# Token choice of a state-space and attention block: scores spread by a repeated column, ranks added in one operation, one-hot rows in one comparison

## The chip, the cores and the metric

The kernel runs on one core of a Trainium2 chip (trn2). A core has a matrix engine (PE, with its weight loads listed apart as PEld), VectorE (DVE), ScalarE (ACT), GpSimd (POOL) and SyncE (SP, which here only issues transfers), an on-chip memory SBUF of 128 partitions, and the accumulators PSUM in 8 banks. The engines run their own instruction streams in program order and wait for each other on semaphores. The metric is the device time of one execution in microseconds (us); lower is better.

## What is computed

The input has 4 batches of 512 tokens with 256 features. The first half is a selective state-space layer with 16 states per channel, followed by a layer norm; the second half picks 64 of the 512 tokens of each batch by a router score, runs attention and an MLP over the 256 picked tokens, puts them back, and ends with another layer norm. Cut to what matters for the change:

```
x = layernorm(x + ssm(x))                       # the scan: h = dA * h + dBu, 16 states
scores = einsum('btd,d->bt', x, w_router)       # [4, 512]
_, idx = top_k(scores, 64); idx = sort(idx)     # 64 tokens of each batch, in token order
sel = x[b, idx]                                 # [256, 256], then attention and MLP on it
output = x.at[b, idx].set(gated)
x = layernorm(x + output)
```

The kernel has no sort. A token is picked when fewer than 64 tokens of its batch rank ahead of it; its place among the picked ones is the count of picked tokens in front of it; a 0/1 matrix (the one-hot rows, token by place) then gathers rows by a matmul.

## The kernel before

A batch has 4 chunks (C = 4) of 128 tokens, one token per partition. The scan runs as a loop of 64 steps t, 16 for each of the 4 batches, one state per step. In a step PE turns two blocks of the scan's input into PSUM (`turn_bu`, line 538) and sums weighed states (`add_states`, line 675); ACT makes the decays (line 1037) and most of the scan's input (line 1027); DVE runs two scans of 512 tokens (line 1186); POOL weighs the states (`weigh`, line 1565, 128x1024) and in every second step makes a part of the scan's input (`make_z`, line 1578).

Between these, hand-written tables put the pieces of other work. `FRONT_AT` puts the preparation of the next batch (convolution, projections) into the steps of the current one, and `TAIL_AT` puts the tail of the batch before: its output projection (o0, o1), layer norm (ls, lp, la), router scores (lx), the spreading of scores (ld, sb), ranks (k0 to k3), places (pf), and the gather (ga, and for every second batch the position tables, cs). So the tails of batches 0, 1 and 2 run inside the scan of batches 1, 2 and 3, and the tail of batch 3 (`LAST_TAIL`) runs after the loop, mixed with the first query and key projections (q0 to q11: PE line 699, DVE lines 1329 and 1334, POOL line 1594) and value projections (v0, v1: PE line 709). Each engine takes the pieces in the same order, each piece at its place in that engine's stream.

The pieces that the change touches, in the order in which a tail runs them:

- lx0, lx1 (DVE, line 1250): four sums of products with the router's weights, one for each chunk. They write the scores into column 256 of the chunk's rows in `x1`, and raise `x1_ready` after two chunks and after four.
- ld0, ld1 (POOL, line 1625): four 128x128 diagonal matrices, the identity times a chunk's score column, into `score_diag`; each raises `diag_ready`.
- sb (PE, line 628): two matmuls of all ones with two diagonals each (128x256). Their result in a PSUM bank has on every partition all 512 scores of the batch.
- k0 to k3 (DVE, lines 1263 to 1267): for each chunk up to three comparisons of the 512 scores with the chunk's own, summed into `ranks`, which has three rows of four numbers per partition. Chunk 0 has no number in the first row, so that one is kept at zero.
- The end of k3 (DVE, lines 1274 to 1280): two additions give the rank, `chosen` is 1 where it is below 64 (this releases pf on PE), `offset` is 0 or 1000, and a memset puts the zero back.
- pf (PE, lines 632 and 635, DVE, lines 1284 and 1288): eight records of small matmuls on `chosen` count the picked tokens in front, DVE adds `offset` to make `place`, and four comparisons of `slot_no` (0 to 63) with a chunk's `place` make the one-hot rows, 128x64 each.
- ga, cs (PE, lines 641 and 647): the gather, and the cosines and sines of the picked positions.

Between k3 and pf DVE has the two scans of the next step. PE's queue is in program order too: what stands behind a waiting piece waits with it.

Of the kernel before, what the change touches and what calls it, by code (L numbers as in the profile page):

```python
# [51 lines left out]
FIRST_BU = ("cv0c", "cv0d")  # L52
TAIL_AT = {
    2: ("y0", "y1", "g0", "g1"), 4: ("o0",), 5: ("o1",), 6: ("ls0", "ls1"), 7: ("lp0", "lp1"),
    8: ("la0", "la1"), 9: ("lx0", "lx1", "ld0", "ld1"), 10: ("sb",), 11: ("k0",), 12: ("k1",), 13: ("k2", "k3"),
    14: ("pf",), 15: ("ga", "cs"),
}

# [2 lines left out]
NORM_AT = {5: "hs", 6: "hp", 7: "hr", 8: "ht"}  # L61
LAST_TAIL = (
    "y0", "y1", "g0", "g1", "q0", "q1", "o0", "q2", "ls0", "q3", "lp0", "ls1", "q4", "o1", "lp1", "q5", "q6",
    "la0", "la1", "lx0", "lx1", "ld0", "ld1", "q7", "q8", "sb", "k0", "k1", "k2", "k3", "v0", "q9", "q10", "pf",
    "q11", "ga", "v1", "cs",
)
NO_FILL = (
    "su", "s1", "s2", "s3", "s4", "s5", "s6", "rs", "y0", "y1", "g0", "g1", "ls0", "ls1",
    "la0", "la1", "lp0", "lp1", "lx0", "lx1", "ld0", "ld1", "k0", "k1", "k2", "k3",
)  # L70


# [19 lines left out]
def block_kernel(nc, x, W_in, conv_w, conv_b, W_x, W_dt, b_dt, A_log, D, W_out, w_router, wq, bq, wk, bk, wv, bv,  # L92
# [115 lines left out]
    with ExitStack() as ctx:  # L208
        def sb(name, shape, dt=F32):
            return ctx.enter_context(nc.sbuf_tensor(name, shape, dt))  # L210
# [112 lines left out]
        x1 = sb("x1", [P, B * C, NCOL])  # L323
        junk = sb("junk", [P, 2, L], BF16)
        h_buf = sb("h", [P, ST * DM + KD * S])
        score_diag = sb("score_diag", [P, C, P])
        ranks = sb("ranks", [P, 3, C])
        offset = sb("offset", [P, C])
        chosen = sb("chosen", [P, C])
        place = sb("place", [P, C])  # L330
# [31 lines left out]
        total = loop_buf[:, FC * S:FC * S + B * C * DM].rearrange("p (b c d) -> p b c d", b=B, c=C)  # L362
        out_rows = total
        selT = gT_buf[:].rearrange("p (t l) -> p t l", t=ST)
        change = score_diag[:].rearrange("p a b -> p (a b)").rearrange("p (t d) -> p t d", t=ST)
        h_rows = h_buf[:, 0:ST * DM].rearrange("p (t d) -> p t d", t=ST)
        hT = h_buf[:, ST * DM:].rearrange("p (k s) -> p k s", k=KD)

# [35 lines left out]
        rstd_ready = sem("rstd_ready")  # L404
        rows_ready = sem("rows_ready")
        x1_ready = sem("x1_ready")
        diag_ready = sem("diag_ready")
        chosen_ready = sem("chosen_ready")
        onehot_ready = sem("onehot_ready")
        sel_stat = sem("sel_stat")  # L410
# [125 lines left out]
        def _(pe):  # L536
# [68 lines left out]
            def tail(b, piece):  # L605
                o = int(piece[-1]) if piece[-1].isdigit() else 0
                name = (piece, b)
                if piece in NO_FILL or (piece == "cs" and b % 2 == 0):
                    return
                wait_free(pe, name)  # L610
                t = at(name)
                if piece in ("o0", "o1"):
                    pe.wait_ge(in_w["w_out"], 16)
                    pe.wait_ge(g_ready, 2 * b + o + 1)
                    pe.wait_ge(res_ready, b + 1)
                    for i in range(2):
                        cols = slice((2 * o + i) * P, (2 * o + i + 1) * P)
                        for k in range(KD):
                            mm = pe.matmul(t[:, i * DM:(i + 1) * DM], gT[:, k, cols], w_out_s[:, k, :],  # L619
                                           start=(k == 0), stop=(k == KD - 1))  # L620
                        for k in range(KD):
                            a = i * DM + k * P
                            mm = pe.matmul(t[:, a:a + P], resT[b % 2][:, k, cols], ident[:], start=False,
                                           stop=True, skip_group_check=True)
                elif piece == "sb":
                    for i in range(2):
                        pe.wait_ge(diag_ready, C * b + 2 * (i + 1))
                        mm = pe.matmul(t[:, 2 * P * i:2 * P * (i + 1)], ones[:],
                                       score_diag[:, 2 * i:2 * i + 2, :].rearrange("p c j -> p (c j)"), start=True, stop=True)
                elif piece == "pf":  # L630
                    pe.wait_ge(chosen_ready, b + 1)
                    mm = pe.matmul(t[:, 0:C], before[:], chosen[:], start=True, stop=True)
                    for w in range(1, C):

                        mm = pe.matmul(t[:, w:C], ones[:], chosen[:, 0:C - w], start=False, stop=True,
                                       skip_group_check=True)
                elif piece == "ga":
                    pe.wait_ge(onehot_ready, C * (b + 1))
                    r = K * (b % 2)
                    for c in range(C):  # L640
                        mm = pe.matmul(t[r:r + K, 0:NCOL], onehot[:, b // 2, c, r:r + K], x1[:, C * b + c, :],  # L641
                                       start=(c == 0), stop=(c == C - 1))
                elif piece == "cs":
                    pe.wait_ge(tables, 4)
                    for i, tab in enumerate((cos_tab, sin_tab)):
                        for c in range(C):
                            mm = pe.matmul(t[:, i * P:(i + 1) * P], tab[:, c, :], onehot[:, b // 2, c, :],
                                           start=(c == 0), stop=(c == C - 1))
                fill_done(name, mm)
# [520 lines left out]
        def _(dve):  # L1170
# [60 lines left out]
            def tail(b, piece):  # L1231
# [21 lines left out]
                elif piece in ("k0", "k1", "k2", "k3"):  # L1253
# [17 lines left out]
                        return  # L1271
                    drain_done(name, ins)
                    wait_drained(dve, name)
                    link(dve.tensor_tensor(ranks[:, 0, :], ranks[:, 0, :], ranks[:, 1, :], ALU.add))
                    link(dve.tensor_tensor(ranks[:, 2, :], ranks[:, 0, :], ranks[:, 2, :], ALU.add))
                    dve.tensor_scalar(chosen[:], ranks[:, 2, :], float(K), None, ALU.is_lt).then_inc(chosen_ready, 1)

                    dve.wait_ge(chosen_ready, b + 1)
                    link(dve.tensor_scalar(offset[:], chosen[:], -1000.0, 1000.0, ALU.mult, ALU.add))
                    link(dve.memset(ranks[:, 0, 0:1], 0.0))  # L1280
                elif piece == "pf":

                    wait_filled(dve, name)
                    drain_done(name, dve.tensor_tensor(place[:], at(name)[:, 0:C], offset[:], ALU.add))
                    wait_drained(dve, name)
                    r = K * (b % 2)
                    for c in range(C):
                        dve.tensor_scalar(onehot[:, b // 2, c, r:r + K], slot_no[:], place[:, c:c + 1], None,
                                          ALU.is_equal).then_inc(onehot_ready, 1)

            def layer_norm_stats(rows, first, signal, slot=0):

# [210 lines left out]
        def _(pool):  # L1503
# [93 lines left out]
            def tail(b, piece):  # L1597
# [9 lines left out]
                elif piece in ("lp0", "lp1"):  # L1607
# [3 lines left out]
                    if b >= 1:  # L1611
# [3 lines left out]
                    link(inv_sqrt(rstd[:, 0, chunks], var, LN_EPS))  # L1615
                    pool.tensor_tensor(shift[:, 0, chunks], shift[:, 0, chunks], rstd[:, 0, chunks], ALU.mult)\
                        .then_inc(rstd_ready, 1)
                elif piece in ("ld0", "ld1"):
                    o = int(piece[-1])

                    pool.wait_ge(x1_ready, 2 * b + o + 1)
                    if b >= 1:
                        wait_filled(pool, ("sb", b - 1))
                    for c in range(2 * o, 2 * o + 2):
                        pool.tensor_scalar(score_diag[:, c, :], ident[:], x1[:, C * b + c, DM:DM + 1], 1.0,
                                           ALU.mult, ALU.mult).then_inc(diag_ready, 1)

            for piece in FIRST_FRONT:
                front(0, piece)
# [63 lines left out]
```

## Time and profile before

| | us |
|---|---|
| three timed runs | 489.69, 491.65, 491.72 (median 491.65) |
| the profiled execution | 488.78 |
| its span, first to last instruction | 487.0 |
| PE busy | 413.7 (85%) |
| DVE busy | 313.9 (64%) |
| ACT busy | 294.4 (60%) |
| POOL busy | 284.9 (59%) |

The profile is of one execution. A row of the timeline gives a start, a length, the engine, the line, what is written and read with its shape and count, and in brackets how long the engine had been idle before and what released it. Neighbouring rows of one kind are merged, and a row's end can overlap the next one's start a little, since an operation's last results are still under way. An operation that is held by the hardware after its start shows the wait in its length, not in the brackets. Busy shares are means over stages with different limits, so the reading goes by stage: scan loop to about 345 us, last tail to 384, projections to 399, attention to 447, then MLP and output.

### The profile page before, as it was taken

What the parts mean: (1) busy time and instruction counts of PE and PEld (TensorE: products, weight loads), DVE (VectorE), ACT (ScalarE), POOL (GpSimd) and SP (SyncE); (2) the same over time, 40 slices, a digit from 0 to 9 for tenths busy, and PEclk for the clock granted to TensorE, in tenths of its full rate; (3) what the DMA queues carried; (4) which work ended last, traced back from release to release, by engine and by line L of the source; (5) the groups of instructions that cost most, each with busy time, mean ns of one, the idle gap of its engine ahead of it and who ended that gap; (6) DMA issues with size and microseconds to landing.
All of it is one profiled execution on the core that took longest, in us unless ns stands there. A gap on an engine that the chain in (4) does not pass through costs nothing.

```text
span 487.0 us, 6491 instructions
## 1 busy us (share of the span) xinstructions
PE 413.7 (85%) x2021; PEld 249.4 (51%) x2021; DVE 313.9 (64%) x624; ACT 294.4 (60%) x628; POOL 284.9 (59%) x261
## 2 busy tenths in 40 slices
PE   5989898899999799899875789866968998999991
PEld 3433353444445344446333346342755777888881
DVE  0302664588665579973689967999489396544355
ACT  4255588994786993676795376971252465553152
POOL 2010086678987889777889769996562253331012
PEclk9999999999999979999989699977997899999996
DMA  7102501106101004111002204870400000000013
GB/s 235 44 0 72 148 23 31 34 2 160 59 24 42 23 0 93 64 43 42 7 18 67 89 25 157 250 282 0 174 0 1 2 0 1 3 0 1 1 44 129
DMA packets 18709, 29.10 MB, mean 60 GB/s; under 512 B 2698, under 2 KB 10676, under 8 KB 18420
## 3 DMA queue, kind: packets, MB, share of 16 engines
q1 hardware_dynamic: 18676, 28.70, 19.1%
q8 instruction: 16, 0.26, 0.2%
q14 instruction: 17, 0.14, 0.1%
HBM read 22.27 MB, written 2.23 MB: 50 GB/s over the span
## 4 chain that ended last, share of the span: by engine, by line
PE 45%; ACT 15%; DVE 12%; POOL 8%; issue 8%; POOLq 0%; DVEq 0%; ACTq 0%
PE bank L538 8%; PE bank L554 7%; ACT loop_buf L1027 6%; ACT front_a L1037 5%; PE bank L675 4%; POOL state L1565 3%; PE bank L851 3%; PE bank L827 3%; PE bank L619 2%; PE bank L641 2%; DVE state L1186 2%; PE bank L859 1%; PE bank L576 1%; PE bank L798 1%; PE bank L818 1%
## 5 line engine op out<-in xcount | busy, mean ns | idle before, releaser
L1186 DVE TENSOR_TENSOR_SCAN state<-front_a,bank 128x512 f32<-128x512 f32 x88 | 102.6, 1204 | 42.9 <-PE bank L538 21.3
L538 PEld LDWEIGHTS bank<-ident,loop_buf 128*128 128x128 f32 x512 | 60.4, 146 | 83.5 <-issue 40.1
L538 PE MATMUL bank<-ident,loop_buf 128*128 128x128 f32 x512 | 84.8, 290 | 17.2 <-ACT loop_buf L1027 15.4
L1037 ACT ACTIVATE front_a<-loop_buf,a_neg 128x512 f32<-128x512 f32 x128 | 84.4, 713 | 7.9 <-DVE copy L1186 4.8
L1027 ACT ACTIVATE loop_buf<-copy,b_rows 128x256 f32<-128x256 f32 x190 | 78.9, 496 | 0.1
L554 PE MATMUL bank<-front_c,conv_raw 128*128 128x512 f32 x128 | 60.7, 607 | 2.5 <-ACT front_c L902 0.9
L1186 DVE TENSOR_TENSOR_SCAN copy<-front_a,bank 128x512 f32<-128x512 f32 x40 | 47.1, 1207 | 23.8 <-PE bank L538 8.4
L1565 POOL TENSOR_TENSOR state<-state,front_a 128x1024 f32<-128x1024 f32 x22 | 52.2, 2375 | 9.0 <-DVE state L1186 9.0
L1565 POOL TENSOR_TENSOR state<-state,c_own 128x1024 f32<-128x1024 f32 x22 | 51.9, 2361 | 9.2 <-DVE state L1186 9.0
L675 PE MATMUL bank<-state,fold 128*64 128x512 f32 x176 | 50.7, 656 | 1.5 <-POOL state L1565 1.5
L1578 POOL TENSOR_TENSOR loop_buf<-copy,b_rows 128x512 f32<-128x512 f32 x31 | 33.4, 1079 | 24.4 <-ACT copy L902 21.9
L554 PEld LDWEIGHTS bank<-front_c,conv_raw 128*128 128x128 f32 x128 | 23.0, 195 | 22.9 <-issue 20.8
L1594 POOL TENSOR_TENSOR loop_buf<-state 128x256 f32<-128x256 f32 x24 | 17.5, 732 | 28.0 <-DVE state L1334 28.0
L1538 POOL TENSOR_TENSOR copy<-front_c,front_b 128x1024 f32<-128x1024 f32 x4 | 8.0, 1996 | 35.5 <-ACT front_b L902 30.6
L902 ACT ACTIVATE front_b<-bank,vec 128x512 f32<-128x512 f32 x16 | 10.9, 682 | 29.4 <-PE bank L554 26.3
L902 ACT ACTIVATE copy<-bank 128x512 f32<-128x512 f32 x20 | 11.6, 594 | 27.5 <-PE bank L538 15.3
L1565 POOL TENSOR_TENSOR copy<-copy,c_own 128x1024 f32<-128x1024 f32 x10 | 23.9, 2387 | 5.6 <-DVE copy L1186 5.2
L699 PE MATMUL bank<-h,copy 128*128 128x128 f32 x192 | 23.9, 279 | 1.4 <-ACT h L1044 0.9
L699 PEld LDWEIGHTS bank<-h,copy 128*128 128x128 f32 x192 | 22.5, 193 | 4.3 <-issue 3.0
L1565 POOL TENSOR_TENSOR copy<-copy,front_a 128x1024 f32<-128x1024 f32 x10 | 24.6, 2462 | 0.0
L675 PE MATMUL bank<-copy,fold 128*64 128x512 f32 x80 | 22.5, 641 | 0.4 <-POOL copy L1565 0.4
L1329 DVE SCALAR_TENSOR_TENSOR state<-bank,vec,cosT 128x128 f32<-128x128 f32 x48 | 14.3, 339 | 8.6 <-ACT state L1060 8.5
(205 smaller groups left out, 745.9 us busy)
## 6 DMA issues: line engine op xcount, KB each, us to landing
front_a<-c_stage SPq DMA_DIRECT2D x32, 128.0 KB, 2.9
c_own<-c_stage SPq DMA_DIRECT2D x32, 128.0 KB, 2.8
loop_buf<-front_b SPq DMA_DIRECT2D x32, 128.0 KB, 2.3
copy<-in_L_attn_x SPq DMA_DIRECT2D x4, 512.0 KB, 3.8
front_b<-in_L_ffn_wo SPq DMA_DIRECT2D x1, 2048.0 KB, 10.0
copy<-in_L_ffn_wq SPq DMA_DIRECT2D x1, 2048.0 KB, 8.3
out<-loop_buf SPq DMA_DIRECT2D x3, 512.0 KB, 3.0
conv_raw<-in_L_attn_conv_w SPq DMA_DIRECT2D x2, 512.0 KB, 3.8
```

Of the source, the lines that this page charges most:

```text
L538: return pe.transpose(dst, src, ident[:])
L554: mm = pe.matmul(at(name)[:], conv_x[:, k, i, o * P:(o + 1) * P], xT[:, i, k:k + L], start=(j == 0), stop=(j == TAPS * KD - 1))
L675: mm = pe.matmul(bank[Y_BANK[h]][j * P // 2:(j + 1) * P // 2, :], fold[:], state[t % NH][:, j, :], start=(m == 0), stop=(m == NPAIR - 1))
L699: mm = pe.matmul(at(name)[:, i * P:(i + 1) * P], w_qk[:, k, head * P:(head + 1) * P], hT[:, k, p * P:(p + 1) * P], start=(k == 0), stop=(k ...
L827: mm = pe.matmul(at(("wo", p))[:, 0:DM], oT[:, h, p * P:(p + 1) * P], w_o[:, h, :], start=(h == 0), stop=(h == N_HEADS - 1))
L902: drain_done(name, act.activation(dst, at(name)[:] if src is None else src, func, **kw))
L1027: act.activation(zed[:, g % NZ, c, :, i, :], du_rows[b % 2][:, c, :].rearrange("p (k d) -> p k d", k=2 * KD), ACT.Copy, scale=b_rows[:, b ...
L1037: act.activation(decay[:, u % NDA, :], delta_wide[:, b % 2, k, :], ACT.Exp, scale=a_neg[:, k, m:m + 1]).then_inc(decay_made, 1)
L1186: dve.tensor_tensor_scan(state[t % NH][:, j, :], decay[:, u % NDA, :], bank[BU_BANK[u % NBU]][:], 0.0, ALU.mult, ALU.add).then_inc(scanned, 1)
L1565: pool.tensor_tensor(state[t % NH], state[t % NH], c_wide[g % NCW].unsqueeze(1).to_broadcast([P, 2, L]), ALU.mult).then_inc(weighed, 1)
L1578: pool.tensor_tensor(zed[:, g % NZ, c], rows, cols, ALU.mult).then_inc(z_pool, 1)
L1594: pool.tensor_tensor(qkT[:, 2 * j:2 * j + 2, p * P:(p + 1) * P], qk_raw[:, i0 % NQK], qk_swap[:, i0 % NQK], ALU.add).then_inc(roped, 1)
```

## The change

- The four diagonal matrices of a tail and their pieces ld0 and ld1 go, on POOL. PE makes the spread scores itself: in place of two matmuls of ones with diagonals (128x256) there are four with the score column, read 128 times over with a step of zero, as the stationary operand and the identity as the moving one (128x128 each). PE now waits for `x1_ready`, the scores themselves.
- The two additions of the ranks become one reduction over the three rows of `ranks`, into a tile of its own (`rank_sum`). The zero is then never overwritten, and the memset that restored it goes.
- The four comparisons that make one-hot rows become one, over 128 x 4 x 64, with both operands repeated by steps of zero; it raises `onehot_ready` once.
- `change`, which shared the diagonals' memory, gets a tile of its own. Nothing else reads that memory.

```diff
-    8: ("la0", "la1"), 9: ("lx0", "lx1", "ld0", "ld1"), 10: ("sb",), ...
+    8: ("la0", "la1"), 9: ("lx0", "lx1"), 10: ("sb",), ...
...
                 elif piece == "sb":
-                    for i in range(2):
-                        pe.wait_ge(diag_ready, C * b + 2 * (i + 1))
-                        mm = pe.matmul(t[:, 2 * P * i:2 * P * (i + 1)], ones[:],
-                                       score_diag[:, 2 * i:2 * i + 2, :].rearrange("p c j -> p (c j)"), start=True, stop=True)
+                    for c in range(C):
+                        pe.wait_ge(x1_ready, 2 * b + c // 2 + 1)
+                        mm = pe.matmul(t[:, c * P:(c + 1) * P], x1[:, C * b + c, DM:DM + 1].to_broadcast([P, P]), ident[:],
+                                       start=True, stop=True)
...
                 elif piece == "ga":
-                    pe.wait_ge(onehot_ready, C * (b + 1))
+                    pe.wait_ge(onehot_ready, b + 1)
...
-                    link(dve.tensor_tensor(ranks[:, 0, :], ranks[:, 0, :], ranks[:, 1, :], ALU.add))
-                    link(dve.tensor_tensor(ranks[:, 2, :], ranks[:, 0, :], ranks[:, 2, :], ALU.add))
-                    dve.tensor_scalar(chosen[:], ranks[:, 2, :], float(K), None, ALU.is_lt).then_inc(chosen_ready, 1)
+                    link(dve.tensor_reduce(rank_sum[:], ranks[:].rearrange("p a c -> p c a"), AX.X, ALU.add))
+                    dve.tensor_scalar(chosen[:], rank_sum[:], float(K), None, ALU.is_lt).then_inc(chosen_ready, 1)
...
-                    link(dve.memset(ranks[:, 0, 0:1], 0.0))
...
-                    for c in range(C):
-                        dve.tensor_scalar(onehot[:, b // 2, c, r:r + K], slot_no[:], place[:, c:c + 1], None,
-                                          ALU.is_equal).then_inc(onehot_ready, 1)
+                    shape = [P, C, K]
+                    dve.tensor_tensor(onehot[:, b // 2, :, r:r + K], slot_no[:].unsqueeze(1).to_broadcast(shape),
+                                      place[:].unsqueeze(2).to_broadcast(shape), ALU.is_equal).then_inc(onehot_ready, 1)
...
-                elif piece in ("ld0", "ld1"):
-                    o = int(piece[-1])
-
-                    pool.wait_ge(x1_ready, 2 * b + o + 1)
-                    if b >= 1:
-                        wait_filled(pool, ("sb", b - 1))
-                    for c in range(2 * o, 2 * o + 2):
-                        pool.tensor_scalar(score_diag[:, c, :], ident[:], x1[:, C * b + c, DM:DM + 1], 1.0,
-                                           ALU.mult, ALU.mult).then_inc(diag_ready, 1)
```

DVE at the end of the ranks in batch 1's tail, between the scans of batch 2 (line 1186), before and then after:

```order
L1267 SCALAR_TENSOR_TENSOR junk,ranks<-bank,x,earlier 128x128
L1274 TENSOR_TENSOR ranks<-ranks 128x4
L1275 TENSOR_TENSOR ranks<-ranks 128x4
L1276 TENSOR_SCALAR chosen<-ranks 128x4
L1279 TENSOR_SCALAR offset<-chosen 128x4
L1280 MEMSET ranks 128x1
L1186 SCALAR_TENSOR_TENSOR copy<-front_a,bank 128x512 x2
L1284 TENSOR_TENSOR place<-bank,offset 128x4
L1288 TENSOR_SCALAR onehot<-slot_no,place 128x64 x4
```

```order
L1267 SCALAR_TENSOR_TENSOR junk,ranks<-bank,x,earlier 128x128
L1274 TENSOR_REDUCE rank_sum<-ranks 128x4
L1275 TENSOR_SCALAR chosen<-rank_sum 128x4
L1278 TENSOR_SCALAR offset<-chosen 128x4
L1186 SCALAR_TENSOR_TENSOR copy<-front_a,bank 128x512 x2
L1282 TENSOR_TENSOR place<-bank,offset 128x4
L1286 TENSOR_TENSOR onehot<-slot_no,place 128x4x64
```

The scans stand where they stood; five instructions ahead of them are three, and the four behind `place` are one.

POOL in batch 2's tail, in the scan of batch 3, before and then after (line numbers are two lower after):

```order
L1565 TENSOR_TENSOR state<-state,front_a 128x1024
L1578 TENSOR_TENSOR loop_buf<-copy,b_rows 128x512
L1625 TENSOR_SCALAR score_diag<-ident,x 128x128 x4
L1565 TENSOR_TENSOR state<-state,front_a 128x1024
L1565 TENSOR_TENSOR copy<-copy,front_a 128x1024
```

```order
L1563 TENSOR_TENSOR state<-state,front_a 128x1024
L1576 TENSOR_TENSOR loop_buf<-copy,b_rows 128x512
L1563 TENSOR_TENSOR state<-state,front_a 128x1024
L1563 TENSOR_TENSOR copy<-copy,front_a 128x1024
```

The weighing of the next step follows directly on the make_z, with no wait for the scores between.

## Rows read from the trace of the kernel before

**Rows 1.** Page, part 4: the chain that ended last, by engine.
```profile
PE 45%; ACT 15%; DVE 12%; POOL 8%; issue 8%; POOLq 0%; DVEq 0%; ACTq 0%
```
**Rows 2.** Table by stretch: length; busy PE, PEld, DVE, ACT, POOL; clock; DMA; GB/s.
```profile
272.00:280.00 8.00, 5.77 (x15) 2.45 (x15) 7.96 (x10) 1.45 (x2) 5.07 (x4) 0.50 0.22 78
```
**Rows 3.** Timeline of DVE, batch 0's tail: start, length, line, operation, idle before.
```profile
196.27 4.79 DVE L1288 TENSOR_SCALAR onehot<-slot_no,place 128x64 f32<-128x64 f32 x4
```
**Rows 4.** Timeline of POOL, batch 0's tail.
```profile
174.12 1.04 POOL L1547 TENSOR_SCALAR front_c<-front_c 128x1024 f32<-128x1024 f32 x1 [1.52 <-ACT front_b L981]
...
195.17 2.36 POOL L1565 TENSOR_TENSOR copy<-copy,c_own 128x1024 f32<-128x1024 f32 x1
```
**Rows 5.** Timeline of PE, batch 0's tail.
```profile
177.14 1.13 PE L628 MATMUL bank<-score_diag,ones 128*128 128x256 f32 x4
...
201.21 1.92 PE L641 MATMUL bank<-x,onehot 128*64 128x257 f32 x8 [1.65 <-DVE onehot L1288]
```
**Rows 6.** Timeline of DVE, batch 1's tail.
```profile
263.91 1.46 DVE L1274 TENSOR_TENSOR ranks<-ranks 128x4 f32<-128x4 f32 x1
265.40 2.29 DVE L1275 TENSOR_TENSOR ranks<-ranks 128x4 f32<-128x4 f32 x1
...
270.05 0.96 DVE L1279 TENSOR_SCALAR offset<-chosen 128x4 f32<-128x4 f32 x1
...
271.22 2.33 DVE L1186 TENSOR_TENSOR_SCAN copy<-front_a,bank 128x512 f32<-128x512 f32 x2
...
273.64 3.67 DVE L1288 TENSOR_SCALAR onehot<-slot_no,place 128x64 f32<-128x64 f32 x4
```
**Rows 7.** Timeline of POOL, batch 1's tail.
```profile
262.99 2.35 POOL L1557 TENSOR_TENSOR copy<-front_b,copy 128x1024 f32<-128x1024 f32 x1
...
273.70 2.40 POOL L1565 TENSOR_TENSOR copy<-copy,c_own 128x1024 f32<-128x1024 f32 x1 [0.40 <-PE bank L538]
...
279.63 2.34 POOL L1565 TENSOR_TENSOR copy<-copy,c_own 128x1024 f32<-128x1024 f32 x1 [2.53 <-DVE copy L1186]
285.01 2.37 POOL L1565 TENSOR_TENSOR state<-state,front_a 128x1024 f32<-128x1024 f32 x1 [3.04 <-DVE state L1186]
```
**Rows 8.** Timeline of PE, batch 1's tail.
```profile
277.46 3.66 PE L641 MATMUL bank<-x,onehot 128*64 128x257 f32 x8 [1.94 <-DVE onehot L1288]
...
282.11 1.06 PE L647 MATMUL bank<-onehot,sin_tab 128*128 128x128 f32 x8
```
**Rows 9.** Timeline of DVE, batch 2's tail.
```profile
315.77 2.57 DVE L1250 CUSTOM_DVE_ANT_0 junk<-x,router 128x256 bf16<-128x256 f32 x1
...
319.45 0.42 DVE L1250 CUSTOM_DVE_ANT_0 junk<-x,router 128x256 bf16<-128x256 f32 x1
...
336.92 2.83 DVE L1288 TENSOR_SCALAR onehot<-slot_no,place 128x64 f32<-128x64 f32 x4
```
**Rows 10.** Timeline of POOL, batch 2's tail.
```profile
319.22 1.84 POOL L1625 TENSOR_SCALAR score_diag<-ident,x 128x128 f32<-128x128 f32 x4
```
**Rows 11.** Timeline of PE, batch 2's tail.
```profile
339.90 3.06 PE L641 MATMUL bank<-x,onehot 128*64 128x257 f32 x7 [2.35 <-DVE onehot L1288]
```
**Rows 12.** Timeline of DVE, last tail.
```profile
366.75 0.75 DVE L1265 TENSOR_SCALAR_CACHE_REDUCE z<-bank,x 128x512 bf16<-128x512 f32 x1 [0.30 <-PE bank L628]
...
371.06 0.16 DVE L1274 TENSOR_TENSOR ranks<-ranks 128x4 f32<-128x4 f32 x1
...
372.04 0.61 DVE L1329 SCALAR_TENSOR_TENSOR state<-bank,vec,cosT 128x128 f32<-128x128 f32 x2
...
374.55 1.30 DVE L1288 TENSOR_SCALAR onehot<-slot_no,place 128x64 f32<-128x64 f32 x4
```
**Rows 13.** Timeline of PE, last tail.
```profile
376.00 2.89 PE L641 MATMUL bank<-x,onehot 128*64 128x257 f32 x8 [2.21 <-DVE onehot L1288]
```
**Rows 14.** DVE groups by form: count, busy us, mean ns, idle before.
```profile
L1295 DVE BATCH_NORM_STATS2 stats<-z 128x6 f32<-128x256 f32 x16 | 5.8, 406 | 1.2 <-ACT z L902 1.2
...
L1421 DVE TENSOR_TENSOR state<-state,sel 128x256 f32<-128x256 f32 x2 | 0.8, 424 | 0.0
```

More of the change, by code:

```diff
@@ L54 @@
     2: ("y0", "y1", "g0", "g1"), 4: ("o0",), 5: ("o1",), 6: ("ls0", "ls1"), 7: ("lp0", "lp1"),
-    8: ("la0", "la1"), 9: ("lx0", "lx1", "ld0", "ld1"), 10: ("sb",), 11: ("k0",), 12: ("k1",), 13: ("k2", "k3"),
+    8: ("la0", "la1"), 9: ("lx0", "lx1"), 10: ("sb",), 11: ("k0",), 12: ("k1",), 13: ("k2", "k3"),
     14: ("pf",), 15: ("ga", "cs"),
@@ L63 @@
     "y0", "y1", "g0", "g1", "q0", "q1", "o0", "q2", "ls0", "q3", "lp0", "ls1", "q4", "o1", "lp1", "q5", "q6",
-    "la0", "la1", "lx0", "lx1", "ld0", "ld1", "q7", "q8", "sb", "k0", "k1", "k2", "k3", "v0", "q9", "q10", "pf",
+    "la0", "la1", "lx0", "lx1", "q7", "q8", "sb", "k0", "k1", "k2", "k3", "v0", "q9", "q10", "pf",
     "q11", "ga", "v1", "cs",
@@ L68 @@
     "su", "s1", "s2", "s3", "s4", "s5", "s6", "rs", "y0", "y1", "g0", "g1", "ls0", "ls1",
-    "la0", "la1", "lp0", "lp1", "lx0", "lx1", "ld0", "ld1", "k0", "k1", "k2", "k3",
+    "la0", "la1", "lp0", "lp1", "lx0", "lx1", "k0", "k1", "k2", "k3",
 )
@@ L325, in block_kernel @@
         h_buf = sb("h", [P, ST * DM + KD * S])
-        score_diag = sb("score_diag", [P, C, P])
+        change_buf = sb("change", [P, ST * DM])
         ranks = sb("ranks", [P, 3, C])
+        rank_sum = sb("rank_sum", [P, C])
         offset = sb("offset", [P, C])
@@ L364, in block_kernel @@
         selT = gT_buf[:].rearrange("p (t l) -> p t l", t=ST)
-        change = score_diag[:].rearrange("p a b -> p (a b)").rearrange("p (t d) -> p t d", t=ST)
+        change = change_buf[:].rearrange("p (t d) -> p t d", t=ST)
         h_rows = h_buf[:, 0:ST * DM].rearrange("p (t d) -> p t d", t=ST)
@@ L406, in block_kernel @@
         x1_ready = sem("x1_ready")
-        diag_ready = sem("diag_ready")
         chosen_ready = sem("chosen_ready")
```

## Prediction

> **What bounds the kernel now.** I read the page's chain first: no engine holds it; PE has 45%, the others take turns [rows 1]. So the question is, for each of the four tails, who waits for the pieces that change. For that I read the timelines of DVE, POOL and PE side by side around each tail, looking at idle times in brackets and at operations far longer than their work.
>
> Two things stand out. First, in all four tails PE stands idle in front of the gather, released by DVE's one-hot rows: 1.65, 1.94, 2.35 and 2.21 us [rows 5, 8, 11, 13]. Second, small DVE operations take the time of a POOL operation. A 128x4 addition took 0.16 us in the last tail [rows 12] and 2.29 us in batch 1's, where POOL was working without a pause; the first addition there ends, at 265.4, when POOL's operation from 262.99 does (265.34) [rows 6, 7]. The four comparisons should take well under 1 us; they took 4.79, 3.67, 2.83 and 1.30 [rows 3, 6, 9, 12]. Each such operation seems to wait until the POOL operation then running ends, and POOL's next one goes ahead of DVE's next: one POOL operation (about 2.35 us for a weighing) for each DVE operation. Not every DVE operation is held: the bn_stats of the same loop, one SBUF input of 256, mean 406 ns over 16 of them, which leaves no room for a hold [rows 14]. So the count of held DVE operations is the price, and the change lowers it.
>
> In batch 1's tail this is the bound: DVE is 7.96 of 8 us busy from 272 to 280 while PE, ACT and POOL wait [rows 2], and POOL, which paces the loop after it, is idle 0.40, 2.53 and 3.04 us, each time released by DVE or PE [rows 7].
>
> **Batch 0's tail.** Removed: four comparisons. Added: one, 128x256 with two SBUF inputs. Its nearest row is a 128x256 tensor_tensor, 0.42 us [rows 14]. It may be held once: the POOL operation running when the comparisons began at 196.27 ends at 195.17 + 2.36 = 197.53 [rows 3, 4], so it is done by 197.95 where the fourth was done at 201.06. PE was free at 201.21 - 1.65 = 199.56 [rows 5], so the gather starts then: **1.65 us**, all of PE's wait and no more. PE holds the chain behind it, so I let this carry through. The diagonals were free here: POOL had another 1.52 us to wait for ACT after them [rows 4]. The two saved additions are worth little here, since DVE had slack until the gather.
>
> **PE's new matmuls.** Four 128x256 records took 1.13 us at full clock [rows 5]; the new piece has eight of 128x128, and eight such took 1.06 [rows 8]. I cost it at nothing. The column read with a step of zero as a weight load has no row; above, I bound it by twice the nearest streaming time (1 us more for a tail, of which only batch 0's and the last would be on the path), below by nothing.
>
> **Batch 1's tail.** From 263.91 to 271.22 DVE spends 7.3 us on five tiny operations, four of them held [rows 6]. After, the reduction takes some 0.2 us if it isn't held, and two held ones are left: `chosen` is done when the first addition was (265.4) and `offset` when the second was (267.7). DVE goes on at 267.8, 3.4 earlier. The two scans (2.25) bring it to 270.1, and the single comparison, held for at most 2.40 [rows 7], ends between 270.6 and 273.0 where the fourth ended at 277.3. PE's gather, which began at 277.46, can begin at 273.1 at the latest: 4.4 earlier. If the shorter gap keeps PE's clock up, the gather itself falls from 3.66, at a granted clock of 0.50 (1.2 GHz), to 1.92 [rows 2, 5, 8], 1.7 more. Behind it POOL becomes late: it has only 0.40 + 2.53 + 3.04 = 5.97 us of idle time to give back [rows 7]. So 4.4 to 6.0. Should the reduction be held as the addition was, everything up to the one-hot is one operation (2.3) later: 4.4 - 2.3 = 2.1. Ends 2.1 and 6.0; I take **5.3**, since bn_stats, the nearest row for a reduction along the free axis, is not held.
>
> The Trainium skill ("SBUF — State Buffer", Who interferes with whom) says that on trn2 tensor_reduce never contends with GpSimd, while tensor_scalar and a tensor_tensor with two SBUF inputs do. The held rows here agree; no run shows a reduction from SBUF yet. By that rule the lower end is 4.4, not 2.1.
>
> **Batch 2's tail.** Here POOL's diagonals stood on the chain: 1.84 us [rows 10]. But DVE's four router sums overlap them, and they are held too: 2.57 against 0.42 us for the fourth, which ran at 319.45 beside the diagonals [rows 9]. Without these, POOL starts the next weighing at 319.2, and by the alternation the fourth sum waits for it: 2.35 us later, and DVE with three scans behind it is the later engine from there. So the removal is not a gain but a loss: **-2.35** if held (nearest: the second sum), 0 if it slips in. Then the rank part, unheld: two operations fewer, 0.4 us (five take 0.98 in the last tail [rows 12]). Then the comparison: POOL is idle there, waiting for the scan; the first of four ran at once and the rest waited for the weighing it let start. A single one goes at once: 2.83 - 0.42 = 2.4, and PE's wait was 2.35 [rows 9, 11]. Sum -2.35 + 0.4 + 2.4 = **0.45**; ends 2.8 (sum not held) and -1.95 (the comparison held as well).
>
> **Last tail.** PE's spread no longer waits for POOL, but DVE, busy with query projections until then, had waited just 0.30 us [rows 12]; that is all that can be gained there. The rank part saves 0.4. The comparisons: 1.30 becomes 0.42, or some 1.0 if held by the short POOL addition that held the first: 0.3 to 0.9. Sum 1.0 to 1.6; I take **1.2**. PE's wait of 2.21 covers it [rows 13], and the stage behind starts from PE, so it carries to the end.
>
> Against the merging speaks the Trainium skill ("VectorE: DVE Perf Modes", The perf-mode tier table): fp32 tensor_scalar streams two elements a cycle, tensor_tensor one. By its 0.96 GHz that is, as an estimate, 0.13 us more streaming for 256 elements. The rows decide otherwise: the operations cost mostly what is fixed and what holds them, not the streaming.
>
> **The sum.** 1.65 + 5.3 + 0.45 + 1.2 = 8.6 us. Against the profiled execution (488.78, span 487.0 and 1.8 around it) that is 480.2; that execution lay 2.9 below the median of the timed runs. From the median, 491.65 - 8.6 = 483.0, which I forecast.
>
> **Rivals.**
> - *Slower: the sums collide everywhere.* In batches 0 and 1 too POOL could run on into its next work once the diagonals are gone, and DVE's four router sums would be held as in batch 2: some 2 us each, 8 a tail, 16 for two tails. It decides at line 1547, which follows the diagonals: for it POOL must be free of its wait for ACT, which lasted 1.52 us past the diagonals in batch 0 [rows 4]. Against: that wait is ACT's, and the change does nothing for ACT. Time: 491.65 - 8.6 + 16 = 499.
> - *Given back in the loop.* ACT or PE turns out to pace the scan, so that what tails 0 and 1 free is waited for elsewhere; 0.45 + 1.2 remain: 490.0. Against: POOL's idle times name DVE and PE as releasers. For: ACT and PE hold much of the chain between the tails.
> - *The low ends.* The reduction is held (2.1), the sum and the comparison in batch 2 are both held (-1.95), and the last gives 1.0: 1.65 + 2.1 - 1.95 + 1.0 = 2.8, so 488.9. The part of the change that adds ranks then does little of what it should.
> - *The high ends.* 1.65 + 6.0 + 2.8 + 1.6 = 12.05: 479.6.
>
> **How the numbers follow.** Forecast 0.53 (481 to 486), high ends 0.18, low ends 0.14, given back 0.11, collision 0.04. A measurement tells about 0.5%, 2.5 us, from no change; the forecast, the high ends and most of the low ones lie beyond. Faster 0.81, same 0.15, slower 0.04. The range of 8 in 10 leaves out the collision and what is given back, and takes in most of the low ends and, for the 2.9 between profile and median, a little beyond the high ones: 478.5 to 488.5.
>
> **What would show it.** Per tail in the profile after: no wait of PE in front of batch 0's gather; in batch 1 a reduction of 0.2 us and two held operations behind it, POOL's idle sum of 6 us nearly gone; in batch 2 a fourth router sum over 2 us long, and the comparison at its bare 0.4; in the last tail a gather some 1.2 us nearer to the end of the scan. Wrong it would be if the reduction takes 2 us beside POOL, if the column's weight loads take much over 0.25 us, or if POOL's idle times reappear further on.

## The result, and the profile after

The changed kernel takes 476.25 us (median of 6 runs, 473.71 to 479.89) where the kernel before, on the same chip, has 490.85. The ratio is 0.9706, 95% interval 0.9648 to 0.9765: 14.6 us less. In a second comparison it was 0.9718 (0.9686 to 0.9751), 13.7 us. Medians here and below are of all executions; ratios and their intervals are of those within 1.5% of the fastest execution of the same kernel. The forecast was 8.6 us less, and its range ended at 478.5: the direction is right, the size too small. The profiled execution took 478.12 (span 476.4, mean clock 0.952) beside 488.78 (487.0, 0.943).

DVE of the changed kernel in the four tails, answering [rows 3, 6, 9, 12] (start, length, line, operation, idle before):

```profile
198.64 1.70 DVE L1286 TENSOR_TENSOR onehot<-slot_no,place 128x256 f32<-128x256 f32 x1
...
264.87 0.17 DVE L1274 TENSOR_REDUCE rank_sum<-ranks 128x4 f32<-128x12 f32 x1
265.07 0.99 DVE L1275 TENSOR_SCALAR chosen<-rank_sum 128x4 f32<-128x4 f32 x1
266.10 2.29 DVE L1278 TENSOR_SCALAR offset<-chosen 128x4 f32<-128x4 f32 x1
...
271.54 0.42 DVE L1286 TENSOR_TENSOR onehot<-slot_no,place 128x256 f32<-128x256 f32 x1
...
313.47 2.55 DVE L1250 CUSTOM_DVE_ANT_0 junk<-x,router 128x256 bf16<-128x256 f32 x1
...
332.17 0.43 DVE L1286 TENSOR_TENSOR onehot<-slot_no,place 128x256 f32<-128x256 f32 x1
...
366.35 0.42 DVE L1286 TENSOR_TENSOR onehot<-slot_no,place 128x256 f32<-128x256 f32 x1
```

In batch 1 the reduction is not held, and the two small operations behind it are. The single comparison is held once, in batch 0, and takes its bare 0.42 us, as [rows 14] had it, in the other three. The fourth router sum of batch 2 is long, where it took 0.42 before.

POOL of the changed kernel, answering [rows 7], with the DVE scans that wait for PE behind batch 1's gather:

```profile
263.67 2.36 POOL L1555 TENSOR_TENSOR copy<-front_b,copy 128x1024 f32<-128x1024 f32 x1
...
271.60 2.59 POOL L1563 TENSOR_TENSOR state<-state,c_own 128x1024 f32<-128x1024 f32 x1
274.14 2.35 POOL L1563 TENSOR_TENSOR copy<-copy,c_own 128x1024 f32<-128x1024 f32 x1
...
277.63 3.44 DVE L1186 TENSOR_TENSOR_SCAN state<-front_a,bank 128x512 f32<-128x512 f32 x3 [2.31 <-PE bank L538]
...
285.97 2.51 POOL L1604 TENSOR_TENSOR gT<-gT,copy 128x512 f32<-128x512 f32 x2 [0.49 <-DVE gT L1239]
...
366.39 0.97 POOL L1592 TENSOR_TENSOR loop_buf<-state 128x256 f32<-128x256 f32 x1 [0.55 <-DVE state L1332]
```

From 263.67 to 285.5 POOL has no idle time left. PE has none from 266.18 to 279.6 either, and DVE's scans wait 2.31 us for it: both engines are full in this stretch now.

PE's four gathers and the projection behind the last, answering [rows 5, 8, 11, 13]:

```profile
201.90 1.90 PE L641 MATMUL bank<-x,onehot 128*64 128x257 f32 x8
...
273.27 1.90 PE L641 MATMUL bank<-x,onehot 128*64 128x257 f32 x8
...
332.74 2.78 PE L641 MATMUL bank<-x,onehot 128*64 128x257 f32 x7
...
366.92 1.92 PE L641 MATMUL bank<-x,onehot 128*64 128x257 f32 x8 [1.16 <-DVE onehot L1286]
368.78 1.98 PE L709 MATMUL bank<-front_c,h 128*128 128x512 f32 x4
```

Three of the four waits for DVE's one-hot rows are gone. And the gathers are shorter themselves: 1.90 for 3.66 in batch 1, 1.92 for 2.89 in the last tail, where the projection took 2.66 before. That is PE's clock: the granted clock over the gather was 0.50 in batch 1 and 0.64 in the last tail (0.74 over the projection), and it is 1.00 over all three now. Batch 2's gather is still at 0.64. PE's 32 weight loads from the repeated column took 185 to 338 ns (median 191) where the 16 from `ones` took 186 to 337 (median 238): no price.

Where the time went, tail by tail, from the starts of the same scan operation (line 1186) in both traces, and from the end:

| stretch | forecast | changed, profiled |
|---|---|---|
| to the first scan (58.51 before, 61.07 after) | 0 | -2.6 |
| batch 0's tail | 1.65 | 1.84 |
| batch 1's tail | 5.3 | 6.68 |
| batch 2's tail | 0.45 | 1.35 |
| last tail | 1.2 | 3.3 |
| the tails together | 8.6 | 13.2 |

The first row isn't the change. It comes and goes between executions: the rank part alone, which touches nothing there, started its first scan at 61.09, and one of the kernels below that holds the whole change, at 58.73. A second profiled execution of the changed kernel (475.64 us) gave 3.4, 7.1, 1.4 and 3.3 us in the four tails, so a tail can differ by 1.6 between executions. The question is why the tails gave 13.2 and not 8.6.

The chain of the page names less than half of the span now, so its shares can't be set beside [rows 1] one by one; PE still holds the most of it:

```profile
PE 23%; DVE 10%; ACT 5%; POOL 3%; issue 3%; POOLq 0%; DVEq 0%; ACTq 0%
```

### The profile page after: what moved, and what is told of

The parts are those of the page before. It is cut to its first block and busy times, and to the rows that moved or that the text cites. A ratio compares the mean times of both kernels' runs of the same rounds, so it can differ in the third digit from the quotient of the medians.

```text
span 476.4 us, 6481 instructions
## 1 busy us (share of the span) xinstructions
PE 413.1 (87%) x2037; PEld 250.5 (53%) x2037; DVE 302.2 (63%) x604; ACT 294.5 (62%) x628; POOL 278.7 (59%) x245
## 5 line engine op out<-in xcount | busy, mean ns | idle before, releaser
L538 PE MATMUL bank<-ident,loop_buf 128*128 128x128 f32 x512 | 85.0, 291 | 16.2 <-ACT loop_buf L1027 14.6
```

What stands on the lines that cost most here:

```text
L538: return pe.transpose(dst, src, ident[:])
```

## The experiments

### Each part alone, and each part undone

The diff has three parts that can be applied one by one: the rank addition (lines 1274 to 1280), the single comparison (line 1288), the spread scores without diagonals (lines 628 and 1625).

Rank part alone:

```
-  ranks0 += ranks1; ranks2 += ranks0; chosen = ranks2 < K; ...; memset
+  rank_sum = tensor_reduce(ranks); chosen = rank_sum < K; ...
```

> The kernel before with the rank part alone: one reduction for two additions, no memset. Theory (a DVE operation on two SBUF inputs, or a comparison of SBUF data, is held until POOL's running operation ends; a reduction is not): in batch 1's tail chosen and offset stay held, the scan behind them starts 3.4 us earlier, the four comparisons are still held; batch 2 and the last tail gain 0.4 each. 3 to 5 us faster than before. Rival (the reduction is held like the addition): its row in batch 1's tail is over 1 us long and the gain is 1 to 2 us.

Measured: 490.95, ratio 0.9992 (0.9963 to 1.0022). A miss: nothing is gained that can be measured. Its trace, batch 1's tail, DVE, then POOL and PE:

```profile
265.55 0.17 DVE L1275 TENSOR_REDUCE rank_sum<-ranks 128x4 f32<-128x12 f32 x1
265.75 1.17 DVE L1276 TENSOR_SCALAR chosen<-rank_sum 128x4 f32<-128x4 f32 x1
266.95 2.28 DVE L1279 TENSOR_SCALAR offset<-chosen 128x4 f32<-128x4 f32 x1
269.27 2.33 DVE L1187 TENSOR_TENSOR_SCAN copy<-front_a,bank 128x512 f32<-128x512 f32 x2
...
272.39 5.97 DVE L1287 TENSOR_SCALAR onehot<-slot_no,place 128x64 f32<-128x64 f32 x4
```

```profile
271.49 1.03 POOL L1577 TENSOR_TENSOR loop_buf<-copy,b_rows 128x512 f32<-128x512 f32 x1
272.49 2.35 POOL L1564 TENSOR_TENSOR state<-state,c_own 128x1024 f32<-128x1024 f32 x1
274.81 2.33 POOL L1564 TENSOR_TENSOR copy<-copy,c_own 128x1024 f32<-128x1024 f32 x1
277.11 1.03 POOL L1577 TENSOR_TENSOR loop_buf<-copy,b_rows 128x512 f32<-128x512 f32 x1
...
278.50 3.66 PE L642 MATMUL bank<-x,onehot 128*64 128x257 f32 x8 [3.93 <-DVE onehot L1287]
```

Up to the scan it went as forecast, 3.5 us sooner. But DVE now comes to the four comparisons when POOL has four operations in a row: the comparisons took 5.97 us, 2.3 more than before [rows 6], and end at 278.36, where POOL's fourth ends at 278.14. PE waits 3.93 us for them. What was saved on held additions was spent on held comparisons.

Single comparison alone:

```
-  for c in range(C): tensor_scalar(onehot[:, c], slot_no, place[:, c], is_equal)
+  tensor_tensor(onehot, slot_no repeated, place repeated, is_equal)
```

> The kernel before with the single comparison alone. Theory: batch 0's gather loses its wait of 1.65 us; batch 1's rank part stays as long as before (7.3 us) and the one-hot rows come 3.3 us earlier; batch 2 gains 2.4, with the diagonals still there and so no held fourth router sum; the last tail gains 0.9, and up to 1.5 more if PE's clock stays up for the gather. 7 to 10 us faster. Rival (the parts are worth something only together, since POOL or ACT paces batch 1): under 5 us.

Measured: 479.49, ratio 0.9763 (0.973 to 0.9796), 11.3 us; more than expected, and what the excess is was not followed up.

Spread scores alone:

```
-  ld0, ld1: POOL score_diag = ident * score; PE sb: ones x score_diag, 128x256 x4
+  PE sb: (score column repeated) x ident, 128x128 x8
```

> The kernel before with the spreading of scores alone (no diagonals, the column as stationary operand). Theory: nothing in batches 0 and 1; in batch 2 the fourth router sum is held by a weighing (2.5 us long instead of 0.42), which costs 2.1 us; the last tail gains 0.45. So 1 to 2.5 us slower than before. Rival (the diagonals stood on the chain, 1.84 us in batch 2, and PE's wait of 4.78 us in the last tail was theirs): 2 to 5 us faster.

Measured: 492.49, ratio 1.0037 (1.0004 to 1.0071): a loss of about 1.7, as expected.

The whole change once more, in the same comparison:

> The whole change, beside its parts on the same chip. By the theory the parts add up nearly: 3 to 5, 7 to 10 and -1 to -2.5, so 10 to 13 us faster than before; the first measurement had 14.6. Rival (the parts need each other): the whole is over 3 us more than the sum of the parts measured beside it.

Measured: 477.05, ratio 0.9718 (0.9686 to 0.9751), as expected, 13.7 us. The parts alone sum to 9.4: some 4 us belong to no part alone. So each was undone from the changed kernel. Four comparisons back:

> The changed kernel with the four comparisons back (ranks by one operation and spread scores stay). Theory (whatever time DVE saves ahead of them, the four comparisons lose again, since each waits for one of POOL's operations): nothing is left of the change, 490 to 493, with a one-hot of 5 to 6 us in batch 1's tail where the changed kernel has 0.42. Rival (the parts simply add): the single comparison's 11.3 go and the rest stays, 488 or a little less.

Measured: 492.08, ratio 1.0001 (0.9972 to 1.0029). As the theory has it: without the single comparison nothing is left. (Its profiled execution was the shortest of its 12; the one-hot of batch 1 took 4.58 us there, under the expected 5 to 6.) The old rank additions back:

> The changed kernel with the rank additions back (single comparison and spread scores stay). Theory (with the single comparison the two held additions are a loss of their own): batch 1's scan resumes some 3.4 us later than in the changed kernel, of which POOL's idle time behind covers a part; 479.5 to 481, about 2.5 to 4 over the changed kernel. Rival (rank part worth nothing as it is alone): 476.5 to 477.5.

Measured: 479.67, ratio 0.9756 (0.9724 to 0.9788): by the medians 2.6 to 3.4 us over the changed kernel, as the theory has it. DVE in its batch 1:

```profile
262.36 1.18 DVE L1274 TENSOR_TENSOR ranks<-ranks 128x4 f32<-128x4 f32 x1
263.57 2.28 DVE L1275 TENSOR_TENSOR ranks<-ranks 128x4 f32<-128x4 f32 x1
265.89 2.29 DVE L1276 TENSOR_SCALAR chosen<-ranks 128x4 f32<-128x4 f32 x1
268.21 0.96 DVE L1279 TENSOR_SCALAR offset<-chosen 128x4 f32<-128x4 f32 x1
...
271.80 0.42 DVE L1288 TENSOR_TENSOR onehot<-slot_no,place 128x256 f32<-128x256 f32 x1
```

Four held operations ahead of the scan, one free comparison behind it. The diagonals back (rank part and single comparison together):

> The rank part and the single comparison together, the scores spread by POOL's diagonals as before. Alone they were worth -0.2 and 11.3 us. Theory (the rank part's gain needs the single comparison: with four, the time saved on held additions is lost again on comparisons held by POOL's work, 5.97 us against 3.67): together they give 11.3 and some 2.5 to 3 for batch 1's tail, and the spreading is a loss also here (2.15 in batch 2, less 0.3 and 0.4): 475 to 476, a little under the whole change. Rival (the rank part gives nothing, and the whole change's extra over the sum of its parts came with the spreading): 479 to 480.

Measured: 477.41, ratio 0.9704 (0.9646 to 0.9762): 1.4 to 2.4 more than expected, and the same as the whole change. Beside the other two, the spreading is worth nothing that can be measured. So the rank part is worth 0 alone and 2 to 3 us with the single comparison. By the ratios it is 0.9756 beside 0.9706 and 0.9718 (1.9 to 2.5 us), and 0.9763 beside 0.9704 (2.9 us). The intervals of each pair overlap, but all 12 executions with the single comparison alone or with the spread scores have a mean of 479.7, and the 16 that have the rank part too 476.9. In the traces, batch 1's tail gives 3.7 us with the old additions and 6.7 without.

### The router sums of batch 2

The prediction put 2.35 us of loss on the fourth router sum, held by the weighing that the missing diagonals let start sooner. Two kernels make POOL wait for the sums, with one line in its tail, the first ahead of the weighing after the make_z, the second two operations earlier:

```
+  if b == 2: pool.wait_ge(x1_ready, 2 * (b + 1))
```

> The changed kernel with one wait more: in batch 2's tail POOL starts the weighing that follows the make_z only when all four router sums are there. Theory (the fourth sum is held by that weighing, a loss of 2.15 us in the changed kernel): the sum takes 0.4 us instead of 2.55, the scan behind it comes some 2.1 us sooner, and POOL, which stands idle 2.68 us two operations later, loses nothing: about 474.5 where the changed kernel has 476 to 477. Rival (the sum is long because of PE's new reads of the same score columns, not because of POOL): it stays at 2.5 us and the time at 476 to 477.

> The changed kernel with the same wait put two POOL operations earlier, so that in batch 2's tail the third and fourth sums and mostly the second too run with POOL idle. Theory: each of them then takes 0.4 instead of 2.57, 1.25 and 2.55 us, DVE is through the four some 5 us sooner, and the scan behind them with it; POOL starts two operations up to 1.5 us later, for which its idle 2.68 and 0.60 us pay. 471.5 to 473. Rival (POOL, held back by the wait, becomes what the scan waits for): no more than one hold is won, 474 to 475.5.

DVE and POOL with the first wait, then DVE, POOL and PE with the second:

```profile
313.33 0.41 DVE L1250 CUSTOM_DVE_ANT_0 junk<-x,router 128x256 bf16<-128x256 f32 x1
...
313.83 2.36 POOL L1563 TENSOR_TENSOR state<-state,front_a 128x1024 f32<-128x1024 f32 x1 [0.71 <-DVE x L1250]
```

```profile
305.51 0.41 DVE L1250 CUSTOM_DVE_ANT_0 junk<-x,router 128x256 bf16<-128x256 f32 x1
...
305.86 0.41 DVE L1250 CUSTOM_DVE_ANT_0 junk<-x,router 128x256 bf16<-128x256 f32 x1
...
306.20 0.41 DVE L1250 CUSTOM_DVE_ANT_0 junk<-x,router 128x256 bf16<-128x256 f32 x1
...
306.70 2.37 POOL L1563 TENSOR_TENSOR state<-state,front_a 128x1024 f32<-128x1024 f32 x1 [1.40 <-DVE x L1250]
...
320.41 2.28 DVE L1278 TENSOR_SCALAR offset<-chosen 128x4 f32<-128x4 f32 x1
...
325.71 3.23 PE L641 MATMUL bank<-x,onehot 128*64 128x257 f32 x7 [2.31 <-DVE onehot L1286]
...
360.51 3.40 PE L641 MATMUL bank<-x,onehot 128*64 128x257 f32 x8 [1.16 <-DVE onehot L1286]
```

The sums are as the theory has them: 0.41 instead of 2.55, and in the second kernel three times 0.41. The scan behind them starts 2.1 and 5.1 us sooner than in the changed kernel, counted from the last scan ahead of them. The times don't show it: 477.88 (0.969, 0.961 to 0.9771) and 477.3 (0.9718, 0.9652 to 0.9783), the same as the changed kernel. In the second kernel's trace 2.4 of the 5.1 go in the ranks, above all because `offset` is held again, 2.28 us, where POOL had been idle in the changed kernel. Another 0.7 goes at batch 2's gather, 3.23 us for seven matmuls, which at the 0.24 of each of batch 0's eight [rows 5] would be 1.7, and 1.5 at the last tail's, 3.40 where the changed kernel has 1.92. At the end 0.7 is left. In the first kernel's trace 1.3 of the 2.1 go around batch 2's gather, and 0.8 is left at the end. The granted clock over the second kernel's two gathers was 0.50 and 0.56: that pointed to the clock.

### PE's clock

The records give each execution's mean clock. From 36 runs of the kernel before it was 0.945, that is (1 - 0.945) x 2 x 491 = 54 us at the lower of the two levels (1.2 GHz); 12 of the changed kernel had 0.957, 41.5 us. To see what that is worth, PE was kept busy: matmuls of the identity with itself, put in front of PE's waits into a bank that is overwritten next.

```
+  for i in range(n): pe.matmul(bank, ident, ident)   # ahead of the wait
```

First in the kernel before, last tail alone:

> The kernel before with more work for PE and nothing else: in the last tail 18 matmuls of 128x128 ahead of the spread scores and 8 ahead of the gather, in PE's idle times of 4.78 and 2.21 us; their results are overwritten. Theory (of the 3.3 us that the last tail gave, 1.5 are PE's clock: gather 2.89 and the projection behind it 2.66 us where full clock takes 1.92 and 1.98): with PE kept busy both fall to the lower figures and the time by about 1.5 us, 489 beside 490.75. Rival (the clock follows something else): both stay long, 490.75 or a little above.

Measured: 491.0, ratio 0.9992 (0.9956 to 1.0029). A miss in time. In the profiled execution gather and projection did fall, to 2.17 and 1.98 us, but the eight in front of the gather took 3.33 us, the low stretch fell on them (granted clock 0.55), and they ended 1.0 us after the one-hot rows were there. Then in all tails, in both kernels:

> The kernel before with more work for PE and nothing else: 128x128 matmuls (3 to 16 at a place, of about 0.23 us) that fill PE's waits of 1.4 to 4.8 us in front of the spread, the ranks and the gather of all batches and in front of batch 2's du; results are overwritten. The clock in the records says that 36 executions of the kernel before had a mean clock of 0.945, 54 us at the low level, and 12 of the changed kernel 0.957, 41.5 us; within one kernel's executions 1 us less of it goes with 0.15 to 0.45 us less time. Theory (the share of the gain that the sum of operations lacks is PE's clock, kept up by the shorter waits): low time falls by 15 to 25 us and the time by 3 to 6: 485 to 488 beside 491. Rival (the low clock lies beside other work that sets the end): 490 to 492.

> The changed kernel with its own remaining waits of PE filled in the same way (batch 2's du, and spread, ranks and gather of the tails of batches 2 and 3; 3 to 9 matmuls at a place). Theory: low time falls from some 41 to about 25 us and the time by 2 to 4: 473 to 475. Against the filled kernel before, where the clock is then no longer an advantage, the change should be worth less than the 14 us that it gives without: 10.5 to 12.5. Rival (clock of no account): 476.5 to 477.5, and the difference stays at 14.

Measured: 489.26 (0.9969, 0.9928 to 1.0009) and 479.9 (0.9745, 0.9705 to 0.9786). Neither fits. The low time fell as meant, to 30 and 29 us, but one filling stood in the wrong batch. PE of the filled kernel before (L561 is the filling):

```profile
191.60 2.17 PE L561 MATMUL bank<-ident 128*128 128x128 f32 x18
...
267.54 1.06 PE L538 MATMUL bank<-ident,copy 128*128 128x128 f32 x8 [2.96 <-POOL copy L1566]
```

It put 2.17 us on PE's path in batch 0's tail, and the wait of 2.96 it was meant for stayed empty. So once more, with that mended:

> The kernel before with PE's waits filled as in the first filled kernel, but batch 3's du (a wait of 2.95 us ahead of batch 1's ranks) instead of batch 2's (0.69, where the 2.17 us of filling stood on PE's path), and some more in the waits that were still open. The first one ran 1.6 to 2.2 us under the kernel before, in spite of those 2.2. Theory (clock): 3.5 to 5.5 under it, 485.5 to 487.5. Rival (clock of little account, the 2.2 was hidden): 1.5 to 2 under it, 489.

> The changed kernel filled in the same way, with batch 3's du. Theory: without the 2.2 us on PE's path and with the clock up in batch 1's tail and the last: 474 to 476, 1 to 3 under the changed kernel, and 10.5 to 12.5 under the filled kernel before. Rival: the filling delays what comes behind it, 477 to 480 as the first one.

> The changed kernel, filled, and with POOL waiting for all four router sums in batch 2's tail. Theory: the sums' 5 us come through for some 2 to 4 once the gathers behind run at full clock: 471 to 474. Rival (POOL, later by then, or the next low stretch takes it back): 474 to 477.

Measured: 485.64 (0.9875, 0.9828 to 0.9921), 475.73 (0.9665, 0.9612 to 0.9718) and 472.57 (0.961, 0.9565 to 0.9655), with 19 to 20 us of low clock each. All three lie in the ranges expected. Tables by stretch, columns as in [rows 2]; the kernel before, then filled, then the changed one, then filled:

```profile
262.00:290.00 28.00, 19.68 (x98) 11.25 (x100) 23.62 (x32) 13.31 (x28) 21.90 (x12) 0.82 0.28 76
345.00:385.00 40.00, 31.66 (x183) 24.50 (x180) 26.57 (x101) 14.99 (x37) 16.84 (x28) 0.87 0.15 54
```

```profile
262.00:290.00 28.00, 22.73 (x151) 15.55 (x151) 25.49 (x34) 13.53 (x29) 23.78 (x13) 1.00 0.29 77
345.00:385.00 40.00, 36.77 (x261) 31.24 (x258) 26.28 (x102) 16.26 (x41) 16.87 (x28) 1.00 0.15 54
```

```profile
262.00:290.00 28.00, 23.51 (x130) 13.29 (x127) 23.84 (x34) 18.99 (x41) 27.38 (x15) 0.94 0.39 107
345.00:385.00 40.00, 34.00 (x222) 28.15 (x221) 30.08 (x116) 20.00 (x51) 15.84 (x27) 0.91 0.00 1
```

```profile
262.00:290.00 28.00, 24.44 (x148) 14.61 (x149) 24.81 (x35) 18.58 (x40) 27.78 (x15) 1.00 0.35 96
345.00:385.00 40.00, 37.32 (x276) 32.52 (x275) 29.84 (x115) 20.02 (x52) 15.59 (x26) 1.00 0.00 1
```

PE of the filled kernel before, batch 1's gather and the last tail's:

```profile
276.10 2.56 PE L561 MATMUL bank<-ident 128*64 128x128 f32 x22
279.48 1.95 PE L650 MATMUL bank<-x,onehot 128*64 128x257 f32 x8 [0.81 <-DVE onehot L1297]
...
375.62 1.95 PE L650 MATMUL bank<-x,onehot 128*64 128x257 f32 x8 [0.95 <-DVE onehot L1297]
377.50 1.98 PE L718 MATMUL bank<-front_c,h 128*128 128x512 f32 x4
```

With useless work alone the kernel before wins 5.4 us, and its batch 1 tail 1.8, the gather's 3.66 to 1.95. Between the two filled kernels, where the clock is no advantage of either, the change is worth 485.64 - 475.73 = 9.9 us, a little under the 10.5 to 12.5 expected. So of its 14, about 10 are operations and waits, and about 4 are clock, with some 2 us of uncertainty in the split. The third kernel has the wait for all router sums too, and less filling in batch 2's tail, where the sums come sooner: 3.2 us under the filled changed kernel. Between these two traces the scan behind the sums comes 5.2 us sooner, 2.4 go again where `offset` is held, and 2.8 stay to the end. At 472.57 it is the shortest of all, 3.7 under the changed kernel by the medians, which come from different comparisons.

## Where the prediction was right, and which step failed

The holds went as forecast in all four tails. The step that failed is the term of PE's clock. The sum held at most 0.9 us of it, in batch 1's tail, and nothing in the last one; of the 13.2 us that the tails gave, the filled kernels leave 9.0, so by these executions 4.2 are clock.

**Batch 0** went as worked out: held once, no wait at the gather, 1.84 for 1.65.

**Batch 1: mechanism right, the term mis-sized.** The reduction isn't held: 0.17 us at 264.87, within POOL's operation of 263.67 to 266.03. So the Trainium skill ("SBUF — State Buffer", Who interferes with whom) is borne out where it says that tensor_reduce never contends, and my low end was wrong. `chosen` and `offset` are held, as forecast. The cap was wrong: I let POOL give back 0.40 + 2.53 + 3.04 = 5.97 us, and took 5.3. There was a fourth idle time, a little beyond the rows that I had read. POOL of the kernel before:

```profile
291.98 2.51 POOL L1606 TENSOR_TENSOR gT<-gT,copy 128x512 f32<-128x512 f32 x2 [1.27 <-DVE gT L1239]
```

With it there are 7.24 us, of which 0.49 are left after. So in this execution POOL isn't what ended the gain; PE is, which runs without a pause there. Counted from the scan ahead of the ranks, its gather began 4.9 us sooner, took 1.76 less, and the position tables 0.07 less: the 6.7 that were gained. I had 4.4 at the least for the first and 1.7 for the second, and 5.3 for both. Between the filled kernels, where PE's clock is full in this stretch, POOL is the end: it has 5.4 us of idle time there before the change and 0.1 after, and 5.2 are gained.

**Batch 2: right in both directions, short by 0.9.** The fourth sum is held: the scan behind it came 2.15 later, for 2.35 forecast. The comparison at its bare 0.43 gave the 2.4. Missed: the scans no longer wait behind PE's spread, 0.33, and the rank part gave 0.57 for 0.4. The wait kernels show that the sum's hold is POOL's weighing and not PE's new reads.

**The last tail: the clock has no term, and it is most of the miss.** I had 1.2, from 0.3, 0.4 and 0.3 to 0.9. DVE's one-hot rows came 1.7 sooner (0.42 with no hold, and POOL's addition of 366.39 took 0.97 instead of 0.73). The rest of the 3.3 is PE: 2.89 to 1.92 and 2.66 to 1.98, 1.65 together. I had given batch 1's gather such a term, 1.7, of which the 5.3 that I took above the 4.4 holds 0.9, and none to the last tail, though [rows 13] has a gather of 2.89 beside the 1.92 of [rows 5]. Between the filled kernels' traces the tails differ by 1.3, 5.2, 1.2 and 1.3: 9.0 where my sum without clock has 8.6 - 0.9 = 7.7. The last tail's 1.3 is my 1.2 nearly to the number. By these executions 1.3 of the 4.6 that were missing are operations, and 3.3 clock. The split is that of two executions, and the changed one had more low clock (mean 0.967 beside 0.979, none of it in batch 1's ranks and gather or in the last tail), so the share of the operations may be larger.

**The parts don't add.** The prediction costed each edit against the others' end state and summed. That sum is for all three together, and there the rank part is worth 2 to 3 us. Alone it is worth nothing that can be measured: I expected 3 to 5 for it even after the result, and was wrong, because a held operation that is removed hands its wait to the next held one.

**The rivals.** No collision in other batches (the sums of batches 0 and 1 cost no more in the traces, tails 0 and 1 gain). Nothing was given back in the loop: behind batch 1's tail the 6.0 stand unchanged until batch 2's sums. The high ends (479.6) were the nearest, and still 3 us over; and near by their number alone, since their 2.8 for batch 2 needs a fourth sum that isn't held, and it was.

## What to carry to other kernels

Count the operations that a busy neighbour engine can hold, not their work: merging four into one takes away three waits, but taking away some of several held ones ahead of others may only move the wait along. Before summing, give every matmul behind a shortened wait a clock term, from its rows at either level. A cap read from idle times must follow the engine to the first place where it doesn't wait.

## What was not expected of the hardware

- The hold works in both directions. The comparison of 271.54 began 0.06 us ahead of POOL's weighing of 271.60; it took its bare 0.42, and the weighing 2.59 instead of 2.35. The Trainium skill says so in the same section, "SBUF — State Buffer", Who interferes with whom (issue order decides who blocks); the prediction had only asked by whom DVE is held.
- Low clock is cheap on average and dear in places. 35 us less of it (54 to 19) gave the kernel before 5.4 us, 0.15 us for each. In batch 1's gather the 1.7 went through whole, so most of the rest must have lain where others set the pace, which no run shows place by place.
- Executions of one program differ by more than the parts of the change are worth: 22 of the 23 of the kernel before in one comparison lay between 488.25 and 494.01. With 19 us of low clock, filled, it ranged from 483.99 to 486.88. So a part worth 2 us is read from the traces, not from a median of four.
